# Batch norm's squares about a provisional mean, two output buffers and an early square root, in the last stage of a graph network on one core

## The chip, the cores and the metric

One Trainium2 chip, of which the kernel uses one core. The metric is the device time of the whole kernel in microseconds (us), the median of several executions. One execution was also taken by the hardware profiler; all rows of the trace below come from that one. Engines are called PE (TensorE), DVE (VectorE), ACT (ScalarE), POOL (GpSimd) and SP (SyncE, which here only issues transfers).

## What is computed

Three attention layers (GATv2) and then one edge-conditioned convolution (GINE), over a graph of 6,250 nodes with 64 channels and 200,000 edges sorted by destination. The change touches only the end of the last part, which is this:

```
agg = segment_sum(relu(x[src] + edge_attr @ W_edge.T + b_edge), dst)
h = x + agg
h = h @ W1.T + b1                    # 6250 x 64
mean = jnp.mean(h, axis=0)
var = jnp.var(h, axis=0)
h = gamma * (h - mean) * jax.lax.rsqrt(var + BN_EPS) + beta
h = jax.nn.relu(h)
out = x_before + (h @ W2.T + b2)
```

## The kernel before

Nodes lie on 128 partitions by 49 columns. They are worked on in seven groups (GROUPS = 7) of seven blocks (GB = 7) of 128 nodes. Edges are handled in 98 turns per layer; the three attention layers and the convolution each run through all of them. There is no scheduler: each engine has its own program, written out by hand, and the engines meet at semaphores. An engine runs its program in the order in which it is written, so a wait holds back all that stands behind it on that engine.

What follows the last turn is called the end stage here. It has two parts.

**First part, by groups, as gathers come in.** POOL issues 49 indirect transfers (L465), one per block, that fetch each node's summed messages. When the seven of a group have landed, DVE adds them to `h` (L1295, semaphore `s_z`). PE turns the group's seven blocks (L620, "T" below, semaphore `s_zT`, into `pT`, which is the first half of the PSUM tensor `pG`). ACT copies them to `zT` (L644 with output `sb_wide`, two instructions of 512 and 384 columns, "C", semaphore `s_zTc`). PE multiplies by W1 (L626, "M", semaphore `s_u`, into `pP`, the second half of `pG`). ACT adds the bias and writes `uT` (L870, two instructions, "I", semaphore `s_uc`). `zT` and `uT` both lie in the tensor `sb_wide`.

**Second part, over all nodes.** DVE sums `uT` by groups (L1304, seven instructions, and L1305 for the last column of the first 27 blocks), sums the sums (L1306) and scales them to minus the mean (L1310, semaphore `s_mean`). ACT squares `uT` about that mean into `zT`, a group at a time (L876, "S", semaphore `s_sq`); DVE sums the squares in the same way and scales them (L1313). ACT takes the root (L878), DVE makes the scale and bias (L1315 to L1319), ACT applies them with ReLU, seven instructions (L882). PE multiplies each group by W2 (L636, into `pT`); DVE adds the input and the second bias (L1324, two instructions a group, semaphore `s_final`), and SP sends the group's rows out (L456). PE's product of group g waits until DVE is done with group g - 1, since both use `pT`.

On DVE's program the seven additions L1295 stand in one loop, and the loop of L1304 behind it:

```
for g in range(GROUPS):
    sl = slice(g * GB, (g + 1) * GB)
    dve.wait_ge(s_nrow[g], (LAYERS + 1) * (16 * GB))
    tt(h[:, sl, :], h[:, sl, :], node_rows[:, sl, 0:C], ALU.add).then_inc(s_z, 1)
```

Of the kernel before, what the change touches and what calls it, by code (L numbers as in the profile page):

```python
# [36 lines left out]
P = 128  # L37
N, C, H, O = 6250, 64, 4, 16
# [12 lines left out]
GB = 7  # L51
GROUPS = B // GB
# [15 lines left out]
EPS = 1e-5  # L68
SLOPE = 0.2
LAST_PAD = N - (P - 1) * B  # L70


def build(nc, t):
    with ExitStack() as ctx:
        def sb(name, shape, dt=F32):
            return ctx.enter_context(nc.sbuf_tensor("sb_" + name, shape, dt))

        def sem(name):
            return ctx.enter_context(nc.semaphore(name))
# [29 lines left out]
        with ExitStack() as early:  # L109
# [16 lines left out]
        at = PARTS * B * TW  # L126
# [23 lines left out]
        w2t = sb("w2t", [C, C])  # L150
# [59 lines left out]
        zT = wide[0:C, 0:NB]  # L210
        uT = wide[0:C, NB:2 * NB]

        pG = ctx.enter_context(nc.psum_tensor("pG", [P, 4, 512], F32))
        pT, pP = pG[:, 0:2, :], pG[:, 2:4, :]
        pB = ctx.enter_context(nc.psum_tensor("pB", [P, 2048], F32))
        xr = pB[:, 0:C * G].rearrange("p (c g) -> p c g", g=G)
        at = C * G
# [8 lines left out]

        hT = xl[0:C, 0].rearrange("p g c -> p (g c)")[:, 0:GB * P].rearrange("p (i q) -> p i q", i=GB)
        bn = sb("bn", [C, 10])
        group_sum = sb("group_sum", [C, GROUPS + 1])


        s_x, s_const, s_dst, s_weights = sem("x_in"), sem("constants_in"), sem("dst_in"), sem("weights_in")
# [41 lines left out]
        s_u, s_uc, s_sq, s_bnstd, s_bnp, s_y = (sem(n) for n in (  # L274
            "u_product", "u_copied", "u_squared", "bn_std_ready", "bn_params", "y_ready"))
        s_mean = sem("mean_ready")
        s_o, s_final, s_result = sem("o_product"), sem("final_ready"), sem("result_out")
# [257 lines left out]
        def _(pe):  # L535
# [61 lines left out]
            with pe.Fori(0, PAIRS) as i:  # L597
                for k in range(2):
# [7 lines left out]
                    for q in range(2):  # L606
                        product = pe.matmul(pE[:, q * 512:(q + 1) * 512], attr[:, k, q * P:(q + 1) * P], w_blk[:, :],
                                        start=True, stop=True)
# [6 lines left out]
            for g in range(GROUPS):  # L615
# [3 lines left out]
                for i in range(GB):  # L619
                    product = pe.transpose(place(pT, i)[0:C, :], h[:, g * GB + i, :], ident[:, :])  # L620
# [4 lines left out]
                for half, (lo, n) in enumerate(((0, 4), (4, 3))):  # L625
                    product = pe.matmul(pP[0:C, half, 0:n * P], w1t[:, :], zT[:, (g * GB + lo) * P:(g * GB + lo + n) * P],  # L626
                                        start=True, stop=True)
                product.then_inc(s_u, 1)

            for g in range(GROUPS):  # L630
                pe.wait_ge(s_y, g + 1)
                if g:
                    pe.wait_ge(s_final, g)
                for i in range(GB):
                    b = g * GB + i
                    product = pe.matmul(pT[:, i // 4, (i % 4) * P:(i % 4) * P + C], zT[:, b * P:(b + 1) * P], w2t[:, :],  # L636
                                        start=True, stop=True)
                product.then_inc(s_o, 1)

# [2 lines left out]
        def _(act):  # L642
            def copy(out, in_):
                return act.activation(out, in_, ACT.Copy)  # L644
# [76 lines left out]
            def hand_out_linear(all_done, stored, turn, k):  # L721

                act.wait_ge(s_sums, all_done)
                act.wait_ge(s_stored[k], stored)
                rows = turn_out[:, k].rearrange("p g r -> p (g r)")[:, 0:G * C]
                copy(rows.rearrange("p (g c) -> p g c", g=G), lin_run[:, :, 1:G1].rearrange("p c g -> p g c")).then_inc(s_out, 1)
                act.wait_ge(s_out, all_done)
                act.dma_start(agg_runs[:, bass.ds(turn * (G * C), G * C)], rows).then_inc(s_stored[k], 16)
# [132 lines left out]
                linear_turn(PAIRS - 1, k, last=True)  # L861
            hand_out_linear((LAYERS + 1) * TURNS, (LAYERS + 1) * (16 * PAIRS) - 16, TURNS - 1, 1)

            for g in range(GROUPS):
                act.wait_ge(s_zT, g + 1)
                copy(zT[:, g * GB * P:(g * GB + 4) * P], pT[0:C, 0, :])
                copy(zT[:, (g * GB + 4) * P:(g + 1) * GB * P], pT[0:C, 1, 0:3 * P]).then_inc(s_zTc, 1)
                act.wait_ge(s_u, g + 1)
                for half, (lo, n) in enumerate(((0, 4), (4, 3))):
                    ins = act.activation(uT[:, (g * GB + lo) * P:(g * GB + lo + n) * P], pP[0:C, half, 0:n * P],  # L870
                                           ACT.Identity, bias=cols[:, 0:1])
                ins.then_inc(s_uc, 1)
            act.wait_ge(s_mean, 1)
            for g in range(GROUPS):
                sl = slice(g * GB * P, (g + 1) * GB * P)
                act.activation(zT[:, sl], uT[:, sl], ACT.Square, bias=bn[:, 2:3]).then_inc(s_sq, 1)  # L876
            act.wait_ge(s_bnstd, 1)
# [2 lines left out]
            for g in range(GROUPS):  # L880
                sl = slice(g * GB * P, (g + 1) * GB * P)
# [4 lines left out]
        def _(dve):  # L886
            tt, ts, cp, red = dve.tensor_tensor, dve.tensor_scalar, dve.tensor_copy, dve.tensor_reduce
# [7 lines left out]
            done, last, steps = chain(dve, s_pro)  # L895
# [348 lines left out]
            done, last, steps = chain(dve, s_pro, prologue_steps)  # L1244
# [47 lines left out]
            for g in range(GROUPS):  # L1292
                sl = slice(g * GB, (g + 1) * GB)
# [3 lines left out]
            u3 = uT.rearrange("c (b q) -> c b q", b=B)  # L1297
            z3 = zT.rearrange("c (b q) -> c b q", b=B)

            def node_sum(v3, ready):  # L1300

                for g in range(GROUPS):
                    dve.wait_ge(ready, g + 1)
                    done(red(group_sum[:, g:g + 1], v3[:, g * GB:(g + 1) * GB, 0:P - 1], AX.XY, ALU.add))  # L1304
                done(red(group_sum[:, GROUPS:], v3[:, 0:LAST_PAD, P - 1], AX.X, ALU.add)); last()  # L1305
                done(red(bn[:, 0:1], group_sum[:, :], AX.X, ALU.add)); last()  # L1306

            dve.wait_ge(s_weights, 16 * 9)
            node_sum(u3, s_uc)
            ts(bn[:, 2:3], bn[:, 0:1], -1.0 / N, None, ALU.mult).then_inc(s_mean, 1)  # L1310
            dve.wait_ge(s_mean, 1)
            node_sum(z3, s_sq)
            ts(bn[:, 4:5], bn[:, 0:1], 1.0 / N, EPS, ALU.mult, ALU.add).then_inc(s_bnstd, 1)  # L1313
            dve.wait_ge(s_bnstd, 2)
            done(dve.reciprocal(bn[:, 6:7], bn[:, 5:6])); last()  # L1315

# [3 lines left out]
            for g in range(GROUPS):  # L1320
                dve.wait_ge(s_o, g + 1)
                for half, (lo, n) in enumerate(((0, 4), (4, 3))):
                    sl = slice(g * GB + lo, g * GB + lo + n)
                    ins = tt(XR[:, sl, :], pT[:, half, 0:n * P].rearrange("p (i q) -> p i q", i=n)[:, :, 0:C], x[:, sl, :], ALU.add)  # L1324
                ins.then_inc(s_final, 1)


# [49 lines left out]
```

## Time and profile before

| | us |
|---|---|
| median of 3 executions | 6918.15 |
| lowest, highest | 6915.6, 6918.17 |
| the profiled execution, its own time | 6920.11 |
| the profiled execution, span from first to last instruction | 6918.3 |

The profiled execution's own time is 1.8 us above its span (what lies around the first and last instruction) and 2.0 us above the median. PE is busy for 80% of the span, DVE 73%, POOL 70%, ACT 68%, nearly all of it in the turns. The store of the last turn's sums is issued at 6793.6 us, so the end stage has the last 124 us or so, 1.8% of the span.

### The profile page before, as it was taken

Reading aid. Unit: us, or ns where it says so; the run is one execution under the profiler, and the core shown is the slowest. Engines: PE = TensorE matmul, PEld = TensorE weight load, DVE = VectorE, ACT = ScalarE, POOL = GpSimd, SP = SyncE. Lnnn points to the kernel's source line nnn. Section 1 sums busy time; section 2 is a strip of 40 time slices with the busy share of each in tenths; the row PEclk is TensorE's granted clock in tenths of the full one; section 3 lists DMA queues with packets and bytes.
Section 4 is the critical chain, followed back from the end, with each engine's and each line's share of the span. In section 5 each row is a group of like instructions: output and inputs, shape, how many; then the busy total and the mean of one; then the engine's idle time right before and its main releaser. Section 6 shows DMA issues by size and latency. Waiting matters only on the chain.

```text
span 6918.3 us, 90892 instructions
## 1 busy us (share of the span) xinstructions
PE 5522.5 (80%) x22976; PEld 4471.7 (65%) x22976; DVE 5033.6 (73%) x7664; ACT 4701.4 (68%) x6139; POOL 4844.1 (70%) x5111
## 2 busy tenths in 40 slices
PE   2588888888838888888855888888873999999995
PEld 1466666666627777777744777777762777777773
DVE  7588888888838988888865988888884434343442
ACT  0477777777727888888854888888871555555553
POOL 3666666666667777777767777777765777777774
PEclk9998999989959999999977999999996999999996
DMA  8444545445425555555533555555552444444441
GB/s 362 130 150 150 150 150 149 148 148 149 150 65 158 165 163 164 164 164 164 164 108 113 161 166 162 166 163 164 164 149 60 135 131 135 131 135 130 136 129 44
DMA packets 419825, 1018.62 MB, mean 147 GB/s; under 512 B 162514, under 2 KB 195268, under 8 KB 415446
## 3 DMA queue, kind: packets, MB, share of 16 engines
q1 hardware_dynamic: 198850, 612.23, 26.1%
q0 software_dynamic: 164208, 181.25, 14.2%
q10 hardware_dynamic: 56740, 224.88, 8.1%
q14 instruction: 23, 0.19, 0.0%
q8 instruction: 4, 0.07, 0.0%
HBM read 633.43 MB, written 384.49 MB: 147 GB/s over the span
## 4 chain that ended last, share of the span: by engine, by line
POOL 31%; issue 28%; DVE 18%; ACT 16%; ACTq 2%; PE 2%; DMA 1%; DVEq 1%; POOLq 0%; SPq 0%
POOL sb_xl L465 26%; ACT sb_turn_out L644 7%; DVE pG L1047 7%; DVE sb_s_run L1089 4%; POOL sb_hot_f L465 3%; ACT pB L644 3%; ACT sb_hot L644 3%; ACT sb_v_in L644 2%; POOL marks L469 2%; DVE sb_wide L1039 2%; DVE sb_s L1272 2%; PE pG L553 1%; DVE sb_mark L997 1%; ACT L644 1%; ACTq L718 1%
## 5 line engine op out<-in xcount | busy, mean ns | idle before, releaser
L553 PE MATMUL pG<-sb_xl_parts,sb_hot 128*128 128x476 f32 x21952 | 5187.1, 395 | 1110.5 <-ACT sb_xl L644 675.2
L465 POOL DMA_INDIRECT sb_xl<-xl_table,sb_idx x4704 | 4448.0, 946 | 1702.7 <-issue 1433.9
L553 PEld LDWEIGHTS pG<-sb_xl_parts,sb_hot 128*128 128x128 f32 x21952 | 4273.3, 197 | 2064.5 <-issue 1434.1
L1047 DVE COPY_PREDICATED pG<-sb_pick_turn,pG 128x408 f32<-128x408 int32 (+2 forms) x2352 | 1017.9, 435 | 1082.2 <-ACT sb_pick_turn L644 960.9
L644 ACT ACTIVATE sb_hot<-sb_wide 128x1792 fp32r<-128x1792 bf16 x784 | 1320.2, 1697 | 308.2 <-ACT sb_turn_out L644 287.3
L1089 DVE TENSOR_TENSOR_SCAN sb_s_run<-pB,sb_v_in 128x272 f32<-128x272 f32 (+2 forms) x1075 | 1083.9, 1016 | 24.4 <-ACT sb_turn_out L644 4.0
L644 ACT ACTIVATE sb_turn_out<-sb_s_run 128x1088 f32<-128x1088 f32 (+1 forms) x392 | 835.2, 2131 | 2.6 <-DVE sb_s_run L1089 2.6
L644 ACT ACTIVATE sb_xl<-pG 128x136 f32<-128x136 f32 (+2 forms) x826 | 243.1, 297 | 811.1 <-DVE pG L1047 724.9
L1086 DVE TENSOR_TENSOR_SCAN pB<-sb_same_c,pB 128x1024 f32<-128x1024 f32 x294 | 671.2, 2283 | 0.1
L644 ACT ACTIVATE sb_v_in<-sb_v_g 128x1024 f32<-128x1024 f32 x291 | 595.3, 2046 | 0.0
L644 ACT ACTIVATE pB<-sb_mark 128x960 f32<-128x960 f32 x294 | 551.5, 1876 | 12.4 <-DMA sb_mark<-marks 1.6
L644 ACT ACTIVATE sb_same_c<-sb_same 128x960 f32 (+1 forms) x294 | 306.3, 1042 | 285.9 <-issue 139.1
L1107 DVE TENSOR_TENSOR sb_s<-sb_xl,pB 128x1024 f32<-128x1024 f32 x294 | 357.8, 1217 | 145.7 <-DMA sb_xl<-xl_table,sb_idx 144.1
L1111 DVE TENSOR_REDUCE sb_e_in<-sb_lr 128x64 f32<-128x1024 f32 x294 | 359.1, 1222 | 10.1
L1109 DVE SCALAR_TENSOR_TENSOR sb_lr<-sb_s,pB 128x1024 f32<-128x1024 f32 x294 | 358.9, 1221 | 10.1
L1138 DVE TENSOR_TENSOR sb_v_g<-sb_xl,pB 128x1024 f32<-128x1024 f32 x291 | 355.2, 1220 | 10.0
L1039 DVE TENSOR_SCALAR sb_wide<-sb_wide,sb_code_no 128x512 bf16<-128x512 int16 x686 | 211.8, 378 | 3.7 <-DMA sb_wide<-codes 3.2
L844 ACT ACTIVATE sb_v_in<-sb_s 128x1024 f32<-128x1024 f32 x98 | 199.4, 2034 | 14.5 <-DVE sb_s L1272 1.3
L644 ACT ACTIVATE pB<-sb_same 128x544 f32 (+1 forms) x98 | 62.5, 638 | 211.3 <-DVE sb_s_run L1089 211.3
L469 POOL DMA_INDIRECT marks<-sb_XR,sb_first_edge x147 | 145.1, 987 | 72.5 <-issue 72.5
L644 ACT ACTIVATE sb_v_in<-sb_s_run 128x68 f32<-128x68 f32 (+1 forms) x389 | 125.4, 322 | 98.1 <-DVE sb_s_run L1089 97.8
L732 ACT ACTIVATE pB<-sb_wf_arg 128x576 f32<-128x576 f32 x294 | 187.1, 636 | 0.0
(199 smaller groups left out, 2278.9 us busy)
## 6 DMA issues: line engine op xcount, KB each, us to landing
sb_wide<-hots SPq DMA_DIRECT2D x294, 896.0 KB
state_rows<-sb_turn_out ACTq DMA_DIRECT2D x294, 576.0 KB
sb_mark<-marks SPq DMA_DIRECT2D x294, 512.0 KB
hots<-sb_wide SPq DMA_DIRECT2D x98, 896.0 KB, 4.0
sb_xl<-xl_table,sb_idx POOLq DMA_INDIRECT x4704
marks<-sb_hot_f SPq DMA_DIRECT2D x32, 1568.0 KB
agg_rows<-sb_turn_out ACTq DMA_DIRECT2D x98, 512.0 KB
sb_wide<-codes SPq DMA_DIRECT2D x98, 128.0 KB, 5.8
```

The source lines that it names most:

```text
L465: return pool.indirect_dma_start(out=dst, out_offset=None, in_=table, in_offset=bass.IndirectOffsetOnAxis(ap=index, axis=0))
L469: return pool.indirect_dma_start(out=table, out_offset=bass.IndirectOffsetOnAxis(ap=index, axis=0), in_=src, in_offset=None)
L553: product = pe.matmul(pG[:, a, 0:GB * TW], hot[k][:, m, a * P:(a + 1) * P], xl_part[part][:, m * GB * TW:(m + 1) * GB * TW], start=(m == 0 ...
L644: return act.activation(out, in_, ACT.Copy)
L1039: ins = ts(staged[k][:, m, :], code[k], code_no[:, m:m + 1], None, ALU.is_equal)
L1047: return dve.copy_predicated(rows[:, :, 0:n], over(pick_turn[:, k, stage, lo:hi], n), rows[:, :, at:at + n])
L1086: dve.tensor_tensor_scan(xr_flat, same_c[:].rearrange(flat3), xr_flat, 0.0, ALU.mult, ALU.add).then_inc(s_xr, 1)
L1089: return dve.tensor_tensor_scan(s_run[:, lo:hi, :].rearrange(flat3), factors[:, 0:(hi - lo) * G1], v_in[:, lo:hi, :].rearrange(flat3), 0.0 ...
L1107: tt(s[:], xl[:, k, :, 0:C], xr.rearrange("p c g -> p g c"), ALU.add).then_inc(s_added, 1)
L1109: done(dve.scalar_tensor_tensor(out=lr[:], in0=s[:], scalar=0.0, in1=blocks(a_turn, G), op0=ALU.max, op1=ALU.mult)); steps_done()
L1111: done(red(e_turn.rearrange("p h g -> p g h"), lr[:].rearrange("p g (h o) -> p g h o", h=H), AX.X, ALU.add)); steps_done()
L1138: tt(v_g[:].rearrange("p g (h o) -> p g h o", h=H), xl_heads, weights, ALU.mult).then_inc(s_used[k], 1)
```

## The change

There are three edits, all in the end stage.

1. **Squares.** ACT squares a group in the first part's loop, right after it has written the group's `uT`, about a provisional mean: that of the first group's columns alone (`bn[:, 2:3]`, made by DVE at L1311 from the first group's sum). DVE sums `uT` and the squares of a group in turn, and at the end corrects mean and variance for the provisional mean (L1313 to L1318).
2. **Output buffers.** The product by W2 uses the two halves of `pG` in turn for even and odd groups, and waits for the additions of group g - 2 in place of g - 1.
3. **Early root.** One `Sqrt` on a column of old data (`stat`) is put ahead of ACT's first part, with its result in a place that is overwritten later.

```diff
@@ tensor
             for g in range(GROUPS):
                 pe.wait_ge(s_y, g + 1)
-                if g:
-                    pe.wait_ge(s_final, g)
+                if g >= 2:
+                    pe.wait_ge(s_final, g - 1)
...
+                    at = 2 * (g % 2) + i // 4
-                    product = pe.matmul(pT[:, i // 4, (i % 4) * P:(i % 4) * P + C], zT[:, b * P:(b + 1) * P], w2t[:, :],
+                    product = pe.matmul(pG[:, at, (i % 4) * P:(i % 4) * P + C], zT[:, b * P:(b + 1) * P], w2t[:, :],
@@ scalar
+            act.activation(bn[:, 9:10], stat[0:C, 2, 0:1], ACT.Sqrt)
             for g in range(GROUPS):
                 act.wait_ge(s_zT, g + 1)
                 copy(zT[:, g * GB * P:(g * GB + 4) * P], pT[0:C, 0, :])
...
                 ins.then_inc(s_uc, 1)
-            act.wait_ge(s_mean, 1)
-            for g in range(GROUPS):
+                act.wait_ge(s_mean, 1)
+                act.wait_ge(s_uc, g + 1)
                 sl = slice(g * GB * P, (g + 1) * GB * P)
                 act.activation(zT[:, sl], uT[:, sl], ACT.Square, bias=bn[:, 2:3]).then_inc(s_sq, 1)
             act.wait_ge(s_bnstd, 1)
@@ vector
-            node_sum(u3, s_uc)
-            ts(bn[:, 2:3], bn[:, 0:1], -1.0 / N, None, ALU.mult).then_inc(s_mean, 1)
-            dve.wait_ge(s_mean, 1)
-            node_sum(z3, s_sq)
-            ts(bn[:, 4:5], bn[:, 0:1], 1.0 / N, EPS, ALU.mult, ALU.add).then_inc(s_bnstd, 1)
+            for g in range(GROUPS):
+                for a, (v3, ready) in enumerate(((u3, s_uc), (z3, s_sq))):
+                    dve.wait_ge(ready, g + 1)
+                    done(red(group_sum[:, a, g:g + 1], v3[:, g * GB:(g + 1) * GB, 0:P - 1], AX.XY, ALU.add))
+                    if g == LAST_PAD // GB:
+                        done(red(group_sum[:, a, GROUPS:], v3[:, 0:LAST_PAD, P - 1], AX.X, ALU.add))
+                    if g == 0 and a == 0:
+                        last()
+                        ts(bn[:, 2:3], group_sum[:, 0, 0:1], -1.0 / (GB * (P - 1)), None, ALU.mult).then_inc(s_mean, 1)
+            last()
+            done(red(bn[:, 0:2], group_sum[:, :, :], AX.X, ALU.add)); last()
+            done(dve.scalar_tensor_tensor(out=bn[:, 3:4], in0=bn[:, 0:1], scalar=1.0 / N, in1=bn[:, 2:3], op0=ALU.mult, op1=ALU.add)); last()
+            done(tt(bn[:, 8:9], bn[:, 3:4], bn[:, 3:4], ALU.mult))
+            done(tt(bn[:, 2:3], bn[:, 2:3], bn[:, 3:4], ALU.subtract)); last()
+            done(dve.scalar_tensor_tensor(out=bn[:, 1:2], in0=bn[:, 1:2], scalar=1.0 / N, in1=bn[:, 8:9], op0=ALU.mult, op1=ALU.subtract)); last()
+            ts(bn[:, 4:5], bn[:, 1:2], 1.0, EPS, ALU.mult, ALU.add).then_inc(s_bnstd, 1)
```

What each engine's program holds, before and after, is shown at three places. The first is ACT around the end of the turns. `sb_turn_out` is the last turn's result, `sb_wide` holds `zT` and `uT`, `z_turned` is `s_zT`, `u_product` is `s_u`, `u_copied` is `s_uc` and `mean_ready` is `s_mean`. Before:

```order
L728 DMA agg_rows<-sb_turn_out 128x1024 [waits turn_out_ready]
L644 ACTIVATE sb_wide<-pG 64x512 [waits z_turned]
L644 ACTIVATE sb_wide<-pG 64x384
L870 ACTIVATE sb_wide<-pG,sb_cols 64x512 [waits u_product]
L870 ACTIVATE sb_wide<-pG,sb_cols 64x384
L644 ACTIVATE sb_wide<-pG 64x512 [waits z_turned]
```

Of the change:

```order
L729 DMA agg_rows<-sb_turn_out 128x1024 [waits turn_out_ready]
L865 ACTIVATE sb_bn<-sb_stat 64x1
L645 ACTIVATE sb_wide<-pG 64x512 [waits z_turned]
L645 ACTIVATE sb_wide<-pG 64x384
L872 ACTIVATE sb_wide<-pG,sb_cols 64x512 [waits u_product]
L872 ACTIVATE sb_wide<-pG,sb_cols 64x384
L878 ACTIVATE sb_wide<-sb_wide,sb_bn 64x896 [waits u_copied,mean_ready]
L645 ACTIVATE sb_wide<-pG 64x512 [waits z_turned]
```

The square of the first group, with its wait for `mean_ready`, now stands between the first group's bias (L872) and the second group's copies (L645); the early root stands first. No load of an activation table stands here in either program; the last one is at L829 before and L830 after, ahead of the convolution's turns.

The second place is DVE from the first part's additions on (`sb_hot_f` holds the gathered rows, `sb_group_sum` the sums by group). Before:

```order
L1295 TENSOR_TENSOR sb_h<-sb_h,sb_hot_f 128x448 [waits node_rows_in5]
L1295 TENSOR_TENSOR sb_h<-sb_h,sb_hot_f 128x448 [waits node_rows_in6]
L1304 TENSOR_REDUCE sb_group_sum<-sb_wide 64x1 [waits u_copied,weights_in]
L1304 TENSOR_REDUCE sb_group_sum<-sb_wide 64x1 [waits u_copied] x6
L1305 TENSOR_REDUCE sb_group_sum<-sb_wide 64x1
```

Of the change:

```order
L1297 TENSOR_TENSOR sb_h<-sb_h,sb_hot_f 128x448 [waits node_rows_in5]
L1297 TENSOR_TENSOR sb_h<-sb_h,sb_hot_f 128x448 [waits node_rows_in6]
L1306 TENSOR_REDUCE sb_group_sum<-sb_wide 64x1 [waits u_copied,weights_in]
L1311 TENSOR_SCALAR sb_bn<-sb_group_sum 64x1 [waits dve_prologue_steps]
L1306 TENSOR_REDUCE sb_group_sum<-sb_wide 64x1 [waits u_squared]
L1306 TENSOR_REDUCE sb_group_sum<-sb_wide 64x1 [waits u_copied]
```

The scaling that releases `mean_ready` (L1311) now follows the first sum, where before six more sums stood ahead of it (L1310). The additions of all seven groups still stand ahead of the first sum.

The third place is PE's product by W2 (`y_ready` is counted up by ACT's ReLU, `final_ready` is `s_final`). Before:

```order
L636 MATMUL pG<-sb_w2t,sb_wide 128x64 [waits y_ready]
L636 MATMUL pG<-sb_w2t,sb_wide 128x64 x6
L636 MATMUL pG<-sb_w2t,sb_wide 128x64 [waits final_ready,y_ready]
L636 MATMUL pG<-sb_w2t,sb_wide 128x64 x6
L636 MATMUL pG<-sb_w2t,sb_wide 128x64 [waits final_ready,y_ready]
```

Of the change:

```order
L637 MATMUL pG<-sb_w2t,sb_wide 128x64 [waits y_ready]
L637 MATMUL pG<-sb_w2t,sb_wide 128x64 x6
L637 MATMUL pG<-sb_w2t,sb_wide 128x64 [waits y_ready]
L637 MATMUL pG<-sb_w2t,sb_wide 128x64 x6
L637 MATMUL pG<-sb_w2t,sb_wide 128x64 [waits final_ready,y_ready]
```

The second group's product no longer waits for DVE, and each later one waits for the addition before the last. What surrounds these places stands as it was.

## Rows read from the trace of the kernel before

**Rows 1.** The page: shares of the chain that ended last, by engine

```profile
POOL 31%; issue 28%; DVE 18%; ACT 16%; ACTq 2%; PE 2%; DMA 1%; DVEq 1%; POOLq 0%; SPq 0%
```

**Rows 2.** Timeline: start us, us, engine, instruction, count, idle before; first two groups

```profile
6814.73 0.96 ACT L644 ACTIVATE sb_wide<-pG 64x512 f32<-64x512 f32 x2 [21.22 <-PE pG L620]
...
6819.03 1.15 ACT L870 ACTIVATE sb_wide<-pG,sb_cols 64x512 f32<-64x512 f32 x2 [3.33 <-PE pG L626]
...
6821.43 0.62 DVE L1295 TENSOR_TENSOR sb_h<-sb_h,sb_hot_f 128x448 f32<-128x448 f32 x1 [8.49 <-DMA sb_hot_f<-agg_rows,sb_last_edge]
...
6822.11 1.70 PE L620 MATMUL pG<-sb_ident,sb_h 128*64 128x128 f32 x7 [3.12 <-DVE sb_h L1295]
```

**Rows 3.** Timeline of DVE, PE and ACT from the last group to the ReLU

```profile
6867.14 0.63 DVE L1295 TENSOR_TENSOR sb_h<-sb_h,sb_hot_f 128x448 f32<-128x448 f32 x1 [8.53 <-DMA sb_hot_f<-agg_rows,sb_last_edge]
6867.68 5.99 DVE L1304 TENSOR_REDUCE sb_group_sum<-sb_wide 64x1 f32<-64x889 f32 x6
...
6869.56 0.96 ACT L644 ACTIVATE sb_wide<-pG 64x512 f32<-64x512 f32 x2 [3.71 <-PE pG L620]
...
6870.58 3.24 PE L626 MATMUL pG<-sb_wide,sb_w1t 64*64 64x512 f32 x4 [1.05 <-ACT sb_wide L644]
...
6873.86 1.15 ACT L870 ACTIVATE sb_wide<-pG,sb_cols 64x512 f32<-64x512 f32 x2 [3.33 <-PE pG L626]
...
6876.25 0.15 DVE L1306 TENSOR_REDUCE sb_bn<-sb_group_sum 64x1 f32<-64x8 f32 x1
6876.44 0.14 DVE L1310 TENSOR_SCALAR sb_bn<-sb_bn 64x1 f32<-64x1 f32 x1
6876.62 6.64 ACT L876 ACTIVATE sb_wide<-sb_wide,sb_bn 64x896 f32<-64x896 f32 x7 [1.61 <-DVE sb_bn L1310]
6877.76 6.98 DVE L1304 TENSOR_REDUCE sb_group_sum<-sb_wide 64x1 f32<-64x889 f32 x7 [1.18 <-ACT sb_wide L876]
...
6885.07 0.14 DVE L1313 TENSOR_SCALAR sb_bn<-sb_bn 64x1 f32<-64x1 f32 x1
6885.25 0.20 ACT L878 ACTIVATE sb_bn<-sb_bn 64x1 f32<-64x1 f32 x1 [1.99 <-DVE sb_bn L1313]
...
6886.23 7.28 ACT L882 ACTIVATE sb_wide<-sb_wide,sb_bn 64x896 f32<-64x896 f32 x7 [0.78 <-DVE sb_bn L1319]
```

**Rows 4.** Timeline of PE and DVE in the product by W2

```profile
6887.42 3.25 PE L636 MATMUL pG<-sb_w2t,sb_wide 64*128 64x64 f32 x14 [13.60 <-ACT sb_wide L882]
...
6891.53 3.21 PE L636 MATMUL pG<-sb_w2t,sb_wide 64*128 64x64 f32 x14 [0.87 <-ACT sb_wide L882]
...
6894.79 0.69 DVE L1324 TENSOR_TENSOR sb_XR<-pG,sb_x 128x256 f32<-128x256 f32 x2 [3.40 <-PE pG L636]
...
6911.97 3.21 PE L636 MATMUL pG<-sb_w2t,sb_wide 64*128 64x64 f32 x14 [0.87 <-DVE sb_XR L1324]
```

**Rows 5.** Line L636: duration of one, ns, min/median/max

```profile
L636 PE MATMUL pG<-sb_w2t,sb_wide x98: 417/417/471, 6887.4 to 6914.8; 64*128 64x64 f32 x98
```

**Rows 6.** PE's timeline in the first layer's tables

```profile
50.43 0.64 PE L570 MATMUL pB<-sb_w_gat,sb_xl 64*128 x2
51.01 1.70 PE L564 MATMUL pG<-sb_ident,sb_h 128*64 128x128 f32 x7
```

**Rows 7.** Line L829, the last table load: duration ns, start us

```profile
L829 ACT ACT_TABLE_LOAD  x1: 1283/1283/1283, 5196.7 to 5196.7; - x1
```

**Rows 8.** Windows: busy us of PE, PEld, DVE, ACT, POOL; PEclk; DMA share; GB/s

```profile
5302.00:5308.00 6.00, 5.07 (x13) 4.32 (x14) 4.56 (x3) 1.03 (x1) 5.09 (x4) 0.50 0.09 17
5308.00:5310.00 2.00, 2.00 (x11) 1.76 (x10) 0.00 (x0) 2.00 (x2) 1.70 (x2) 1.00 0.19 35
6749.00:6757.00 8.00, 7.39 (x31) 5.42 (x30) 6.11 (x9) 2.46 (x7) 6.15 (x7) 1.00 0.27 75
6815.00:6819.00 4.00, 3.24 (x4) 0.73 (x4) 0.00 (x0) 0.70 (x2) 2.84 (x4) 0.50 0.11 25
6887.00:6915.00 28.00, 22.35 (x98) 21.39 (x98) 4.13 (x12) 6.51 (x7) 0.00 (x0) 0.50 0.13 49
```

**Rows 9.** Timeline: an edge product in the turns

```profile
6749.43 1.88 PE L607 MATMUL pB<-sb_w_blk,sb_wide 128*128 128x512 f32 x4
```

More of the change, by code:

```diff
@@ L228, in build @@
         bn = sb("bn", [C, 10])
-        group_sum = sb("group_sum", [C, GROUPS + 1])
+        group_sum = sb("group_sum", [C, 2, GROUPS + 1])
         s_x, s_const, s_dst, s_weights = sem("x_in"), sem("constants_in"), sem("dst_in"), sem("weights_in")
@@ L1298, in _ @@
             z3 = zT.rearrange("c (b q) -> c b q", b=B)
-            def node_sum(v3, ready):
-                for g in range(GROUPS):
+            dve.wait_ge(s_weights, 16 * 9)
+            for g in range(GROUPS):
+                for a, (v3, ready) in enumerate(((u3, s_uc), (z3, s_sq))):
                     dve.wait_ge(ready, g + 1)
[L1304 to L1308, printed above, removed]
-            node_sum(u3, s_uc)
-            ts(bn[:, 2:3], bn[:, 0:1], -1.0 / N, None, ALU.mult).then_inc(s_mean, 1)
-            dve.wait_ge(s_mean, 1)
-            node_sum(z3, s_sq)
-            ts(bn[:, 4:5], bn[:, 0:1], 1.0 / N, EPS, ALU.mult, ALU.add).then_inc(s_bnstd, 1)
+                    done(red(group_sum[:, a, g:g + 1], v3[:, g * GB:(g + 1) * GB, 0:P - 1], AX.XY, ALU.add))
[11 more added lines that the diff above has]
+            ts(bn[:, 4:5], bn[:, 1:2], 1.0, EPS, ALU.mult, ALU.add).then_inc(s_bnstd, 1)
             dve.wait_ge(s_bnstd, 2)
@@ L1323, in _ @@
                     sl = slice(g * GB + lo, g * GB + lo + n)
-                    ins = tt(XR[:, sl, :], pT[:, half, 0:n * P].rearrange("p (i q) -> p i q", i=n)[:, :, 0:C], x[:, sl, :], ALU.add)
+                    ins = tt(XR[:, sl, :], pG[:, 2 * (g % 2) + half, 0:n * P].rearrange("p (i q) -> p i q", i=n)[:, :, 0:C], x[:, sl, :], ALU.add)
                 ins.then_inc(s_final, 1)
```

## The prediction, made before the changed kernel had run

> **What bounds the kernel now.** I read the page's chain first, only to see where not to look: of the chain that ended last, 31% is POOL and 28% issue, the gathers of the turns, and the change touches none of it [rows 1]. All three edits lie in the last 124 us, so I read those in order of time, and the question at each edit is who ends the wait there. A change of 0.2% of 6918 us, 13.8 us, is about what a measurement of this kernel can tell from none.
>
> In the first part the gathers set the pace. DVE's addition of the second group waits 8.49 us for a transfer, and PE, behind it, 3.12 us for DVE [rows 2]. ACT is done with the first group at 6819.03 + 1.15 = 6820.18, over a microsecond before the second group's addition starts at 6821.43 [rows 2]. So C, M and I of groups 0 to 5 are hidden under POOL's gathers, and only the last group's are on the path: addition at 6867.14, C at 6869.56, M at 6870.58, I from 6873.86 to 6875.01 [rows 3].
>
> From there the second part is a chain of DVE and ACT: the last sum and its scaling, squares and their sums from 6876.62 to 6884.74, the root, then the ReLU at 6886.23, which is 11.22 us after I [rows 3]. The product by W2 is a ring of PE and DVE: PE starts a group every (6911.97 - 6891.53) / 5 = 4.09 us, works 3.21 and is idle 0.87 while DVE adds for 0.69 [rows 4].
>
> **Edit 1, the squares: first what stands ahead of the new wait.** The first square waits for `s_mean`. L1311 makes it from DVE's first sum, which stands, by DVE's order, behind the additions of all seven groups. The last of those waits for the last gather and starts at 6867.14; the first sum follows at 6867.68 in the trace of before [rows 3], though its data has been there since 6820.18 [rows 2]. Nothing in the change moves it. So L1311 comes at about 6868.8, not early, and ACT stands at its wait from 6820.18 on. Behind that wait on ACT are C and I of groups 1 to 6; behind the second group's C are M of the second group and, on PE's program, T and M of all the later ones. Neither DVE's additions nor POOL wait for ACT here, so the gathers go on as before, and nothing is deadlocked; but the first part, which the gathers hid, now begins again at group 1 when they are over.
>
> The start of that: first sum at 6867.68, 1.06 long (the pass over the squares has seven in 6.98 with the same shape; spaced 0.99), 0.04 to the next instruction (L1306's 0.15 from 6876.25 and L1310 at 6876.44), 0.14 for the scaling, 0.04 to ACT (L876 at 6876.62): S of group 0 at 6868.96 [rows 3]. Seven squares take 6.64, and the isolated one before DVE's sum takes 1.14 to be read (6876.62 to 6877.76), so they are spaced 6.64 less 1.03, over six: 0.935 [rows 3]. C of group 1 starts at 6869.90 and lasts 0.96, M follows 0.06 later (6869.56 + 0.96 to 6870.58): M of group 1 at 6870.92 [rows 3].
>
> One group's step from then on, M to M: M 3.24, 0.04, I 1.15, 0.04 for the new wait on `s_uc`, S 0.935, C 0.96, 0.06, together **6.43 us** [rows 3]. T (1.70, [rows 2]) runs beside I and S, which take 2.17 with their gaps, so it is hidden. If PE needed some 0.15 more ahead of T, as between the last L570 at 50.43 + 0.43 and the next transposes at 51.01 [rows 6], it would still be (1.85 against 2.17). M of group 6 starts at 6870.92 + 5 x 6.43 = 6903.07 and its I ends 4.43 later, at 6907.50. Before it was 6875.01. **Cost: 32.5 us.** The new wait on `s_uc`, which no row shows as such, is the least sure part of a step: between 0, as back-to-back instructions, and 0.2 a time, so the cost lies between 32.3 and 33.5; I take 0.04, as same-engine waits on DVE show.
>
> **What edit 1 gives back.** After the last I, only the last group's square and sum remain: S at 6907.54 for 1.03, sum of squares to 6909.67 (1.06 each; the sum of `uT` runs beside S). Then L1313, of 64x2 where L1306 of 64x1 takes 0.15 [rows 3], and five small operations of which no row shows the three-operand form; as the L1306, L1310 and L1313 rows they take 0.15 and 0.04 between them, one pair without a wait, so that L1318 starts at 6910.55. From L1313 before to the ReLU was 6886.23 - 6885.07 = 1.16 [rows 3], which gives the ReLU at 6911.71: 4.21 us after I, where before it was 11.22. **Gain: 7.0 us**, with bounds 6.0 (each small operation half as dear again and more) and 7.5 (they overlap).
>
> **Edit 2, the output buffers.** DVE's 0.69 leaves the ring. A group has 14 records over 3.21 with the last 0.417 long [rows 4, 5], so they are spaced (3.21 - 0.417) / 13 = 0.215 and 14 of them take 3.01. To that I add the 0.15 at a boundary whose wait is already met [rows 6]: 3.16 a group in place of 4.09. ACT's ReLU (7.28 for seven) and DVE's 0.69 are both shorter than that per group. Six steps: **gain 5.5 us**, with bounds 0 (another wait takes DVE's place) and 6.4 (no gap at all).
>
> **Edit 3, the early root.** What could be gained is a table load, 1.28 us by its row [rows 7]. But the root at L878 takes 0.20 and DVE goes on at once after it, no load stands ahead of it in the trace [rows 3], and the last load is the one at L829 1,690 us earlier [rows 7]. So there is nothing left to load ahead: **0**. The added instruction itself lies in ACT's idle time of 21.22 us before the first C [rows 2]; without that cover it would cost 0.2. The Trainium skill (ScalarE: Activation LUTs, What ACT_TABLE_LOAD costs) gives about 1283 ns for a load, and this trace agrees, 1283; its section on table sets says that cheap functions such as copy and relu are in every set, which fits the root's table staying loaded through the turns. Had a load stood at L878, the sum by that page would be better by 1.3 to 2.7 us, with the drain that it adds.
>
> **The sum.** 32.5 - 7.0 - 5.5 = +20.0 us. On the profiled execution's own time, 6920.1, that is 6940.1; on the median, which lies 2.0 lower, 6918.15 + 20 = **6938 us**, 0.29% slower.
>
> **The rivals.**
>
> *The clock rises (not slower).* The granted clock is 0.50, the 1.2 GHz level, at M and through the whole product by W2, where PE is busy 22.35 of 28 us. It rose to 1.00 (2.4 GHz) at the start of the convolution's turns, after PE had worked without a pause for about 5 us [rows 8]. With two buffers PE works through, and M and T now stand together for 4.94 us in each step. At 1.00 four records of 512 columns take 1.88 [rows 8, 9], M's 1,792 columns so 1.65, 1.6 less than now. If every step of the first part had it, that is 9.6 us; in the product by W2, at half of 3.16 after two slow groups, four steps and the last group, 7.9. Together 20.0 - 17.5: +2.5, **6921**. It decides from 6.2 us on, four fast M's or four fast groups. Against it: in the first layer's tables PE's small products and transposes stand together for about 5 us at a time, and a transpose there takes as long as in the end stage at 0.50: 1.70 for seven both times [rows 2, 6]. I give 4% to both places and 8% to the product by W2 alone, which gives +12.1, **6930**. The Trainium skill (TensorE: Matmul & The Clock Gate, What's actually happening) has it that "the default state is throttled, and activity releases the throttle", which speaks for this rival more than my rows do; by it alone the sum would be that of 6930, or less. For the product by W2 before, at four fifths busy, the trace shows no release.
>
> *The squares do run with the gathers.* If the provisional mean came when the first group's data are there, the 32.5 would go and the rest stay: -12.5, **6906**, or 0.18% faster. It needs DVE's first sum ahead of its later additions, and the order of its program says otherwise. 3%.
>
> *The second buffer gives nothing* (PE's next group is held by something other than DVE): +25.5, **6944**. The 0.87 of idle ends with DVE's addition in every step but the first [rows 4], so 5%.
>
> **How the numbers follow.** My forecast, 6938 with its own range of 6935 to 6941, has 80%. The range from 6930 to 6944 takes in the clock's rise in the product alone and the case without a second buffer's gain, and leaves out the two rivals that hold 7%. Slower by over 0.2%: 80 + 5 and half of the 6930 case, less a little for sizes, 84%. Within 0.2%: the rest of the clock's cases and nearly all of the third rival, 14%. Faster: 2%.
>
> **What the changed kernel's trace would show.** ACT idle for about 48.8 us ahead of its first square, released by DVE's L1311 at about 6868.9; transposes of group 1 done early and its product M 48 us late; M then every 6.4 us; the first sum on DVE right behind the last addition, as now; 4.2 us from the last I to the ReLU; products by W2 every 3.2 us with no idle time on DVE's account; the early root at 0.2 us, no table load. It would be wrong if the square of the first group started before the last gather, or if the clock in the end stage stood at 1.00.

## The result and the profile after

The changed kernel's median is 6935.54 us (6934.06 to 6940.02, 9 runs), that of the kernel before 6915.94 (6913.11 to 6918.41, 9 runs): 19.6 us slower, a ratio of 1.0029 with a 95% interval of 1.0019 to 1.0039. The profiled execution took 6940.02 us, 19.9 more than that of before. The forecast was +20.0 us and, as a time, 6938 us with a range of 6935 to 6941. The measured 6935.54 lies at the lower edge of that range, because the median of the kernel before was 2.2 us lower over nine runs than over the three that the forecast started from.

The timeline of the changed kernel, from the first group to the second square; columns as in [rows 2]:

```profile
6815.86 0.97 ACT L645 ACTIVATE sb_wide<-pG 64x512 f32<-64x512 f32 x2 [20.71 <-PE pG L620]
...
6820.16 1.15 ACT L872 ACTIVATE sb_wide<-pG,sb_cols 64x512 f32<-64x512 f32 x2 [3.33 <-PE pG L626]
...
6867.89 0.63 DVE L1297 TENSOR_TENSOR sb_h<-sb_h,sb_hot_f 128x448 f32<-128x448 f32 x1 [8.50 <-DMA sb_hot_f<-agg_rows,sb_last_edge]
6868.43 1.06 DVE L1306 TENSOR_REDUCE sb_group_sum<-sb_wide 64x1 f32<-64x889 f32 x1
6869.53 0.15 DVE L1311 TENSOR_SCALAR sb_bn<-sb_group_sum 64x1 f32<-64x1 f32 x1
6869.71 1.04 ACT L878 ACTIVATE sb_wide<-sb_wide,sb_bn 64x896 f32<-64x896 f32 x1 [48.40 <-DVE sb_bn L1311]
6870.66 0.94 ACT L645 ACTIVATE sb_wide<-pG 64x512 f32<-64x512 f32 x2
...
6871.66 3.24 PE L626 MATMUL pG<-sb_wide,sb_w1t 64*64 64x512 f32 x4 [46.67 <-ACT sb_wide L645]
...
6874.83 1.70 PE L620 MATMUL pG<-sb_ident,sb_h 128*64 128x128 f32 x7
6874.94 1.15 ACT L872 ACTIVATE sb_wide<-pG,sb_cols 64x512 f32<-64x512 f32 x2 [3.33 <-PE pG L626]
...
6876.18 1.04 ACT L878 ACTIVATE sb_wide<-sb_wide,sb_bn 64x896 f32<-64x896 f32 x1
6877.13 0.95 ACT L645 ACTIVATE sb_wide<-pG 64x512 f32<-64x512 f32 x2
...
6878.13 3.25 PE L626 MATMUL pG<-sb_wide,sb_w1t 64*64 64x512 f32 x4 [1.60 <-ACT sb_wide L645]
```

The bracket of the first L878 is where the cost comes from: ACT stands still for 48.40 us, until DVE's L1311, which starts 1.64 us after the start of the last of the seven additions. Behind it PE stands idle for 46.67 us before its second product by W1, and the first part begins again. From then on the products of two groups start 6.47 us apart.

The end of the same timeline:

```profile
6907.30 1.15 ACT L872 ACTIVATE sb_wide<-pG,sb_cols 64x512 f32<-64x512 f32 x2 [3.34 <-PE pG L626]
6908.48 2.21 DVE L1306 TENSOR_REDUCE sb_group_sum<-sb_wide 64x1 f32<-64x889 f32 x2 [4.27 <-ACT sb_wide L872]
6908.55 1.04 ACT L878 ACTIVATE sb_wide<-sb_wide,sb_bn 64x896 f32<-64x896 f32 x1
6910.73 0.16 DVE L1313 TENSOR_REDUCE sb_bn<-sb_group_sum 64x2 f32<-64x16 f32 x1
...
6911.54 0.15 DVE L1318 TENSOR_SCALAR sb_bn<-sb_bn 64x1 f32<-64x1 f32 x1
6911.72 0.20 ACT L880 ACTIVATE sb_bn<-sb_bn 64x1 f32<-64x1 f32 x1 [2.14 <-DVE sb_bn L1318]
...
6912.71 7.28 ACT L884 ACTIVATE sb_wide<-sb_wide,sb_bn 64x896 f32<-64x896 f32 x7 [0.78 <-DVE sb_bn L1324]
...
6913.89 21.17 PE L637 MATMUL pG<-sb_w2t,sb_wide 64*128 64x64 f32 x98 [6.63 <-ACT sb_wide L884]
6917.18 0.69 DVE L1329 TENSOR_TENSOR sb_XR<-pG,sb_x 128x256 f32<-128x256 f32 x2 [4.51 <-PE pG L637]
...
6935.10 0.69 DVE L1329 TENSOR_TENSOR sb_XR<-pG,sb_x 128x256 f32<-128x256 f32 x2 [2.30 <-PE pG L637]
```

PE's 98 records of the product by W2 (each of the 49 products leaves two) were seven pieces with gaps before, some of them in [rows 4]. Now they are one piece of 21.17 us without a gap.

The two traces laid over each other, in us. The "last gather's addition" is the last L1295 or L1297, at 6867.14 before and 6867.89 after; the "last output addition" is DVE's last L1324 or L1329, at 6915.22 and 6935.10.

| stretch | before | after | difference |
|---|---|---|---|
| start of the last gather's addition to the end of the last I | 7.87 | 40.56 | +32.7 |
| end of the last I to the ReLU | 11.22 | 4.26 | -7.0 |
| ReLU to the start of the last output addition | 28.99 | 22.39 | -6.6 |

That is +19.1. The other 0.8 us of the two profiled executions lie ahead of the last gather's addition, where nothing but the early root was changed; it runs there in ACT's idle time.

### The profile page after: what moved, and what is told of

Same layout as the page of the kernel before. It is cut to its first block, busy times and chain, and to the rows that moved or that the text cites. A ratio compares the mean times of both kernels' runs of the same rounds, so it can differ in the third digit from the quotient of the medians.

```text
span 6938.2 us, 90901 instructions
## 1 busy us (share of the span) xinstructions
PE 5509.4 (79%) x22976; PEld 4465.1 (64%) x22976; DVE 5033.4 (73%) x7667; ACT 4702.2 (68%) x6140; POOL 4841.9 (70%) x5111
## 4 chain that ended last, share of the span: by engine, by line
POOL 31%; issue 28%; DVE 18%; ACT 17%; ACTq 2%; PE 2%; DMA 1%; DVEq 1%; POOLq 0%; SPq 0%
POOL sb_xl L465 26%; ACT sb_turn_out L645 7%; DVE pG L1049 7%; DVE sb_s_run L1091 4%; POOL sb_hot_f L465 3%; ACT pB L645 3%; ACT sb_hot L645 3%; ACT sb_v_in L645 2%; POOL marks L469 2%; DVE sb_wide L1041 2%; DVE sb_s L1274 2%; PE pG L553 1%; DVE sb_mark L999 1%; ACT L645 1%; ACTq L719 1%
## 5 line engine op out<-in xcount | busy, mean ns | idle before, releaser
L645 ACT ACTIVATE sb_hot<-sb_wide 128x1792 fp32r<-128x1792 bf16 x784 | 1320.2, 1697 | 309.0 <-ACT sb_turn_out L645 287.4
L645 ACT ACTIVATE sb_turn_out<-sb_s_run 128x1088 f32<-128x1088 f32 (+1 forms) x392 | 836.6, 2134 | 2.6 <-DVE sb_s_run L1091 2.6
L645 ACT ACTIVATE sb_xl<-pG 128x136 f32<-128x136 f32 (+2 forms) x826 | 242.4, 296 | 808.3 <-DVE pG L1049 723.7
L645 ACT ACTIVATE sb_v_in<-sb_v_g 128x1024 f32<-128x1024 f32 x291 | 595.2, 2045 | 0.0
L645 ACT ACTIVATE pB<-sb_mark 128x960 f32<-128x960 f32 x294 | 551.5, 1876 | 12.8 <-DMA sb_mark<-marks 1.6
L645 ACT ACTIVATE sb_same_c<-sb_same 128x960 f32 (+1 forms) x294 | 306.0, 1041 | 286.6 <-issue 139.4
L645 ACT ACTIVATE pB<-sb_same 128x544 f32 (+1 forms) x98 | 62.5, 638 | 211.3 <-DVE sb_s_run L1091 211.3
L645 ACT ACTIVATE sb_v_in<-sb_s_run 128x68 f32<-128x68 f32 (+1 forms) x389 | 125.6, 323 | 98.4 <-DVE sb_s_run L1091 91.6
```

## The experiments

Times are medians against runs of the kernel before on the same chip; the intervals are those of the ratio. The kernel before took 6915.02, 6915.17 and 6922.15 us on the three chips of these runs, so a time is compared within its chip only. The section ends with a table of all runs by the rows of the end stage.

### Each edit alone

**Squares alone**: edit 1, without the other two. The edit is the squares' part of the diff above.

> Only edit 1 (the squares about the provisional mean), with one output buffer and no early root. My theory: the first square waits on ACT for a DVE sum that stands behind all additions, so groups 1 to 6 start again after the last gather. By the rows of the changed kernel (step 6.47 us from product to product, 21.17 us for the product by W2 in place of about 27.8), this costs about 19.6 + 6.6 = +26 us against the kernel before. The rival that the 19.6 us come from something else in the changed kernel (the buffers or the early root) expects about -7 here.

Measured: 6941.82 against 6915.17 us, **+26.7** (1.0038, 1.0024 to 1.0052; five runs). All of the loss is in this edit, and more than all. ACT's wait before the first square is there without the other two edits:

```profile
6865.27 1.04 ACT L876 ACTIVATE sb_wide<-sb_wide,sb_bn 64x896 f32<-64x896 f32 x1 [47.12 <-DVE sb_bn L1309]
```

**Buffers alone**, edit 2 on the kernel before:

```diff
-                if g:
-                    pe.wait_ge(s_final, g)
+                if g >= 2:
+                    pe.wait_ge(s_final, g - 1)
```

> Only edit 2 (two output buffers). My theory: PE's six steps of 4.09 us become about 2.99, -6.6 us. The rival in which the second buffer helps only behind the slower first part expects 0. The rival in which PE's clock rises, once PE works without a pause, expects -13 or less; the changed kernel's trace speaks against it (0.50 throughout).

Measured: 6908.08 us, **-7.1** (0.9990, 0.9981 to 1.0000). The interval of the time only just ends at 1, so the rows decide:

```profile
6884.42 21.16 PE L637 MATMUL pG<-sb_w2t,sb_wide 64*128 64x64 f32 x98 [13.60 <-ACT sb_wide L883]
```

One piece of 21.16 us, with DVE's additions 2.99 us apart in place of 4.09 and the clock at 0.50 all through. PE's ring loses DVE's part whatever stands ahead of it, and the clock's rival is out. By medians the two edits add up, 26.7 - 7.1 = 19.6, the whole change.

**Root alone**, edit 3 on the kernel before:

```diff
+            act.activation(bn[:, 9:10], stat[0:C, 2, 0:1], ACT.Sqrt)
```

> Only edit 3 (the early root). My theory: 0, within 1.5 us, since no table load stands at the root in the trace. The rival in which a load or its drain is hidden in the root's time expects -1.3 to -2.7; it is near what three rounds can tell, so the root's row and the rows around it decide: I expect 0.20 us for it with and without the early one.

Measured: 6915.70 us, **+0.5** (1.0001, 0.9991 to 1.0010). Times can't tell 0.5 from nothing; the rows can. ACT's timeline with the early root, its last column naming who ended the wait:

```profile
6791.29 0.20 ACT L864 ACTIVATE sb_bn<-sb_stat 64x1 f32<-64x1 f32 x1 [0.41 <-ACT sb_turn_out L644]
...
6880.78 0.20 ACT L879 ACTIVATE sb_bn<-sb_bn 64x1 f32<-64x1 f32 x1 [1.99 <-DVE sb_bn L1314]
6881.76 7.28 ACT L883 ACTIVATE sb_wide<-sb_wide,sb_bn 64x896 f32<-64x896 f32 x7 [0.78 <-DVE sb_bn L1320]
```

The root that matters takes 0.20 us and is followed by the ReLU 0.98 us after its start, both exactly as in [rows 3]. There was no load to take out of the way.

### Is it the order of DVE's program?

**Sums between the additions**: all three edits, but DVE sums group g - 1 right behind the addition of group g.

```diff
+            def group_sums(g):
+                for a, (v3, ready) in enumerate(((u3, s_uc), (z3, s_sq))):
...
             for g in range(GROUPS):
                 sl = slice(g * GB, (g + 1) * GB)
                 dve.wait_ge(s_nrow[g], (LAYERS + 1) * (16 * GB))
                 tt(h[:, sl, :], h[:, sl, :], node_rows[:, sl, 0:C], ALU.add).then_inc(s_z, 1)
+                if g:
+                    group_sums(g - 1)
+            group_sums(GROUPS - 1)
```

> All three edits of the change, with one difference: on DVE the sums of group g - 1 (of u and of its squares, and the first group's scaling) stand right behind the addition of group g, in place of behind all seven additions. My theory: ACT's first square then starts at about 3 us after the first group's bias instead of 48, the first part hides under the gathers again, and the whole change is worth -7.0 - 6.6 = -13.6 us against the kernel before, some 33 us less than the changed kernel. A rival: squares on ACT, 1 us for each group, and DVE's sums, 2 us for each, delay the last group's copies or addition; then it is -10 to -12. If the cost of the change lay not in the order of DVE's program, this kernel would stay at +20.

Measured: 6901.59 us, **-13.6** (0.9980, 0.9971 to 0.9990), and on another chip **-13.6** again, 6901.47 against 6915.02 (0.9980, 0.9971 to 0.9989). The change with its sums moved on one engine goes from 19.6 us slower to 13.6 faster. The first square, and the timeline around the last addition:

```profile
6822.44 1.04 ACT L878 ACTIVATE sb_wide<-sb_wide,sb_bn 64x896 f32<-64x896 f32 x1 [2.51 <-DVE sb_bn L1307]
...
6863.11 1.15 ACT L872 ACTIVATE sb_wide<-pG,sb_cols 64x512 f32<-64x512 f32 x2 [3.33 <-PE pG L626]
6864.35 1.04 ACT L878 ACTIVATE sb_wide<-sb_wide,sb_bn 64x896 f32<-64x896 f32 x1
...
6865.60 0.63 DVE L1312 TENSOR_TENSOR sb_h<-sb_h,sb_hot_f 128x448 f32<-128x448 f32 x1 [6.62 <-DMA sb_hot_f<-agg_rows,sb_last_edge]
6866.15 2.05 DVE L1302 TENSOR_REDUCE sb_group_sum<-sb_wide 64x1 f32<-64x889 f32 x2
```

ACT waits 2.51 us for the provisional mean in place of 48.40. The square of the last group but one is done before the last addition starts, and DVE still waits 6.62 us for a gather there: squares and sums of all groups but the last lie in the gathers' shadow.

**Only the first sum moved**: the first group's sum and L1311 stand behind the second addition, all other sums behind the seventh, as in the changed kernel.

```diff
+                if g == 1:
+                    dve.wait_ge(s_uc, 1)
+                    done(red(group_sum[:, 0, 0:1], u3[:, 0:GB, 0:P - 1], AX.XY, ALU.add)); last()
+                    ts(bn[:, 2:3], group_sum[:, 0, 0:1], -1.0 / (GB * (P - 1)), None, ALU.mult).then_inc(s_mean, 1)
```

> The changed kernel with one DVE pair moved: the first group's sum and the scaling that releases the first square stand behind the second addition; all the other sums stay behind the seventh. My theory: the wait of 48 us goes, and with it the 32.5 us of the restarted first part; in its place 13 sums of about 1 us stand behind the last addition (6867.7), so the ReLU comes some 7.9 us after the last bias in place of 4.2. Against the kernel before: -3.3 - 6.6 = -10 us, about 30 less than the changed kernel. The rival that what counts is to have the sums spread between the additions, not the place of the one wait, expects it near the changed kernel, +20.

Measured: 6912.13 against 6922.15 us, **-10.0** (0.9985, 0.9976 to 0.9995). Against the changed kernel's +19.6, one sum and one scaling, 1.2 us of work, in another place are worth 29.6 us. The first square now waits 3.08 us, and behind the last addition stand the other sums:

```profile
6828.49 1.04 ACT L878 ACTIVATE sb_wide<-sb_wide,sb_bn 64x896 f32<-64x896 f32 x1 [3.08 <-DVE sb_bn L1305]
...
6872.14 0.63 DVE L1301 TENSOR_TENSOR sb_h<-sb_h,sb_hot_f 128x448 f32<-128x448 f32 x1 [8.52 <-DMA sb_hot_f<-agg_rows,sb_last_edge]
6872.68 5.99 DVE L1311 TENSOR_REDUCE sb_group_sum<-sb_wide 64x1 f32<-64x889 f32 x6
...
6879.80 5.99 DVE L1311 TENSOR_REDUCE sb_group_sum<-sb_wide 64x1 f32<-64x889 f32 x6
...
6887.81 7.28 ACT L884 ACTIVATE sb_wide<-sb_wide,sb_bn 64x896 f32<-64x896 f32 x7 [0.78 <-DVE sb_bn L1326]
```

From the last I (6878.86 + 1.15 = 6880.01) to the ReLU it takes 7.80 us, as expected, 3.5 more than the 4.26 with the sums between the additions. That is what the place of the other sums costs.

### The clock in the end stage

The changed kernel's clock stayed at 0.50 through 21 us in which PE never paused. These runs ask why, with products that nobody reads (128x128 weights, 512 columns, into a free part of `pB`), all on the kernel with the sums between the additions.

**Warm in all of the first part**: two extra products behind each product by W1, six behind the last. **Warm at the end**: four behind the last alone.

```diff
                 product.then_inc(s_u, 1)
+                for _ in range(2 if g < GROUPS - 1 else 6):
+                    pe.matmul(pB[:, 0:512], w_blk[:, 0:P], w_blk[:, :], start=True, stop=True)
```

> The kernel with the sums between the additions, with extra products on PE that nobody reads (128x128 weights, 512 columns, into a free part of pB): two behind each group's product by W1, six behind the last. A question about the clock: if work without a pause of the large shape raises it to 1.00 in the end stage and the small products keep it there, the last group's transposes and product by W1 take 2.4 us less and the product by W2 about 10 less, -26 against the kernel before. If the clock falls again in the small products, -14 to -18. If it doesn't rise at all, the six extra products (10.2 us at 0.50) stand in the way of the product by W2 and the kernel is some 3 us slower than without them, -10.

> As the kernel with the sums between the additions, with four extra products (128x128 weights, 512 columns) behind the last group's product by W1 alone, in the time in which PE waits for the batch norm. At 0.50 they take 6.8 us, about the wait. If the clock rises after about 5 us of them and stays: about -8 to -10 against the kernel without them, -22 against the kernel before. If it doesn't rise or falls at once in the small products: 0 to +1 against the kernel without them, -13.

Measured: 6903.99 and 6904.89 against 6922.15 us, **-18.2** (0.9974, 0.9964 to 0.9984) and **-17.3** (0.9975, 0.9965 to 0.9984). Both miss the hopeful numbers, -26 and -22; the second also misses its other case, -13. Windows of the kernel that is warm at the end; columns as in [rows 8]:

```profile
6878.00:6880.00 2.00, 2.00 (x3) 0.75 (x3) 1.07 (x1) 1.88 (x3) 0.00 (x0) 0.50 0.00 0
6880.00:6882.00 2.00, 2.00 (x4) 0.70 (x3) 1.82 (x7) 0.00 (x0) 0.00 (x0) 0.52 0.00 0
6882.00:6884.00 2.00, 1.42 (x4) 0.35 (x2) 0.70 (x5) 1.10 (x2) 0.00 (x0) 1.00 0.00 0
6884.00:6886.00 2.00, 1.71 (x15) 1.71 (x16) 0.00 (x0) 2.00 (x3) 0.00 (x0) 1.00 0.00 0
6886.00:6888.00 2.00, 2.00 (x20) 2.00 (x20) 1.03 (x3) 2.00 (x3) 0.00 (x0) 1.00 0.16 61
6888.00:6890.00 2.00, 2.00 (x15) 2.00 (x14) 0.84 (x4) 2.00 (x3) 0.00 (x0) 0.69 0.46 169
6890.00:6894.00 4.00, 4.00 (x21) 4.00 (x20) 0.89 (x3) 0.39 (x1) 0.00 (x0) 0.50 0.15 57
```

The clock rises at about 6882, 4.3 us after the first extra product (6877.58). In the kernel without the extra products it stays at 0.50 all through the end stage, so they are what raised it. The small ones start at 6884.29, some 20 of them in 2 us where 0.50 allows about nine; and then, with PE busy in every microsecond, the clock falls at about 6889 and stays down to the end of the product by W2. It is not a pause of PE that brings it down here.

**One large product among the small**: one more extra product behind each of the first six groups of the product by W2, added to warm at the end ("keep, end") and to warm in all of the first part ("keep, all").

```diff
                 product.then_inc(s_o, 1)
+                if g < GROUPS - 1:
+                    pe.matmul(pB[:, 0:512], w_blk[:, 0:P], w_blk[:, :], start=True, stop=True)
```

> The kernel with four extra products behind the last product by W1, and one more extra product (128x128 weights, 512 columns) behind each of the first six groups of the product by W2. In the kernel without these six the clock fell from 1.00 to 0.50 about 5 us after the small products had begun, though PE was busy throughout. If what the clock wants is PE's work of the larger shape among the small, it stays at 1.00: seven groups of 1.5 and six extra products of 0.9 take about 16 us in place of 17.1, so about -1 against the kernel without the six, -22 against the sums between the additions is out of reach; about -18 against the kernel before. If it wants only a busy PE, the fall had another cause: the clock falls again, the extra products cost 1.7 each at 0.50, and the kernel is some 5 us slower than without them, -8 against the kernel before.

> All extra products together: two behind each group's product by W1, six behind the last, and one behind each of the first six groups of the product by W2. If the clock stays at 1.00 from the last transposes on: the last group's transposes and product by W1 up to 2.4 us shorter, the product by W2 about 16 us in place of 21.2: -18 to -20 against the kernel before. If it falls in the product by W2: about -12.

> The kernel with the sums between the additions once more, unchanged, on the same chip as the two kernels that add to it, so that the extra products can be weighed against it directly: -13.6 us against the kernel before, the product by W2 at 0.50 throughout in 21.17 us.

Measured against 6915.02 us: keep, all 6898.57, **-16.5** (0.9977, 0.9968 to 0.9986), 2.9 less than the sums between the additions on the same chip. Window of its product by W2, and the timeline of one group and its extra product:

```profile
6879.00:6897.00 18.00, 18.00 (x108) 12.83 (x108) 4.13 (x12) 5.43 (x6) 0.00 (x0) 1.00 0.21 77
```

```profile
6890.24 1.77 PE L639 MATMUL pG<-sb_w2t,sb_wide 64*128 64x64 f32 x14
6891.94 1.12 PE L643 MATMUL pB<-sb_w_blk 128*128 128x512 f32 x2
6893.00 1.77 PE L639 MATMUL pG<-sb_w2t,sb_wide 64*128 64x64 f32 x14
```

In this execution, with a large product among the small, the clock stays at 1.00 to the end. A group with its extra product takes 2.76 us (6890.24 to 6893.00), against 2.99 for the group alone at 0.50.

Keep, end: 6909.94, **-5.1** (0.9986, 0.9977 to 0.9995), but no single number describes it: of 11 executions five took 6896 to 6901 us and six 6910 to 6916. The profiled one is of the second kind. Its timeline of PE:

```profile
6879.34 1.77 PE L639 MATMUL pG<-sb_w2t,sb_wide 64*128 64x64 f32 x14 [1.81 <-ACT sb_wide L888]
6881.04 1.25 PE L643 MATMUL pB<-sb_w_blk 128*128 128x512 f32 x2
6882.23 3.25 PE L639 MATMUL pG<-sb_w2t,sb_wide 64*128 64x64 f32 x14
6885.40 2.07 PE L643 MATMUL pB<-sb_w_blk 128*128 128x512 f32 x2
```

Here PE had paused for 1.81 us between its extra products and the product by W2, and the clock fell during the first extra product of the product by W2, the one behind the first group (1.25 us in place of 1.12). From there a group with its extra product takes 5.18 us. The clock did not come back, though the same mix of products ran without a pause to the end; window of PE from the fall on:

```profile
6882.23:6911.30 29.07, 29.07 (x95) 20.84 (x94) 3.44 (x10) 3.21 (x4) 0.00 (x0) 0.50 0.13 48
```

So the larger shape among the small does not by itself give 1.00: the same mix ran at 1.00 in one execution and at 0.50 in another. The expectation's two cases both occurred, in different executions, the faster five at -15 to -19 us against the kernel before (expected -18), the slower six at -5 to +1 (expected -8). The clock goes with the time: averaged over the whole execution it was 0.919 to 0.920 in the five faster ones and 0.917 or 0.918 in the six slower. Of keep, all one execution in 11 took 6911 us, at 0.919 against 0.920 to 0.922 in the other ten. What decides between the two was not tried.

All runs by their rows: the time from the start of the last gather's addition to the start of DVE's last output addition in the one profiled execution of each, beside the medians.

| kernel | medians, against before | rows, us | against before |
|---|---|---|---|
| before | | 48.08 | |
| the change | +19.6 | 67.21 | +19.1 |
| squares alone | +26.7 | 73.81 | +25.7 |
| buffers alone | -7.1 | 41.47 | -6.6 |
| root alone | +0.5 | 48.08 | 0.0 |
| sums between the additions | -13.6, -13.6 | 34.52, 34.52 | -13.6 |
| only the first sum moved | -10.0 | 38.06 | -10.0 |
| warm in all of the first part | -18.2 | 30.75 | -17.3 |
| warm at the end | -17.3 | 30.48 | -17.6 |
| keep, end (a slower execution) | -5.1 | 45.38 | -2.7 |
| keep, all | -16.5 | 31.38 | -16.7 |

## Why the prediction was right

Point by point, the forecast's terms and what they measured:

| term | forecast | measured |
|---|---|---|
| ACT's wait before the first square | 48.8 us | 48.40 us |
| one step of the restarted first part | 6.43 us | 6.47 us |
| last I, later against the last addition | +32.5 us | +32.7 us |
| last I to ReLU | -7.0 us | -7.0 us |
| ReLU to last output addition (the buffers) | -5.5 us | -6.6 us |
| early root | 0 | 0.0 us by the rows of the root alone |
| sum | +20.0 us | +19.1 us by rows, +19.6 us by medians |

**The wait in front of the first square.** The step that carried the forecast was that L1311 stands behind all seven additions. The run with one sum moved shows it by itself: 29.6 us for one instruction pair in another place.

**What was luck.** The mechanism and the sizes of the first three terms are right, but the sum came nearer than its terms. The buffers gave 1.1 us more than forecast; the profiled executions' difference, 19.9, has 0.8 us back from a stretch ahead of the last gather's addition, and the medians' 19.6 some 0.5 us, which no term stood for.

**The step of 6.43.** It was put together from five durations and their gaps. The new wait on `s_uc`, for which no row stood, I took as 0.04; from the end of the bias to the square it is 0.09 us (6874.94 + 1.15 to 6876.18). That accounts for the 0.04 us by which a step was longer. Transposes were hidden, as said: 6874.83 + 1.70 is before the copies' 6877.13.

**What the edit gives back**: L1313 to L1318 take 0.14 to 0.16 us each with 0.03 to 0.04 between, the forms without a row included; one pair, L1315 and L1316, overlaps, as forecast.

**The buffers.** This term was mis-sized by 1.1 us. I had added 0.15 for the boundary between two groups, read off [rows 6], where the next group's instructions wait for other semaphores. Here 98 records go through at 0.214 us each from the first to the last, and a group takes 2.99 us (DVE's additions 6920.16, 6923.15 and on), not 3.16. The figure without a gap, 3.01, was the right one, and the measured 6.6 us lies just above the upper bound of 6.4 that the forecast gave this term.

**The rivals.** *The clock rises*: it did not, 0.50 over the 98 records and over the steps of 6.47. I had 12% on it, with [rows 2, 6] against it. [rows 6] counts by its durations alone: the profile's clock line reads 1.00 there (see the last section). The Trainium skill (TensorE: Matmul & The Clock Gate, What's actually happening) was in this rival's favour with "activity releases the throttle". The changed kernel does not agree: 21.17 us of PE without a gap stayed at 0.50. The measurement decides.

*The squares run with the gathers*: this is what the kernel with the sums between the additions does. Forecast -12.5, measured -13.6; the 1.1 us between them are the buffers' again. *The second buffer gives nothing*: 7.1 us by itself.

**The early root.** What the forecast's rows left open is why no load stood there. The last load, at L829, belongs to a line that is itself a `Sqrt` (`stat[:, 2, :]`, once ahead of the convolution's turns), and no load follows it in the trace.

## What to carry to other kernels

Before work is moved into a loop that waits for transfers, look in the program of the engine that releases it, not only in that of the engine that does it: an early result counts from when its producer's turn comes. A wait put into the middle of an in-order loop costs everything behind it that had been hidden, here 32.7 us for a wait in front of a square of 1.04 us. The whole change with that producer interleaved is worth 13.6 us, 7.0 of them the squares' by the rows (13.6 less the buffers' 6.6; they were not run without the buffers), so a slower result is no verdict on the idea.

An instruction that loads a table ahead is worth something only if a load stands in the trace at the place that is to be relieved.

## What was not expected of the hardware

**The clock fell under work.** PE's clock fell from 1.00 to 0.50 while PE was busy in every microsecond, in products with 64-row weights and 64 columns: 4.5 us after they began in warm at the end (6884.29 to about 6888.8) and 3.7 us after in warm in all of the first part (6879.57 to about 6883.2). With a product of 128x128 by 512 behind each group it stayed at 1.00 over 18 us in the profiled execution of keep, all. In the turns too, with products of 128x128 by 476, it stood at 1.00 in the window of [rows 8]. But in the profiled execution of keep, end the same mix, once the clock was down, ran for 29 us at 0.50. What the clock went by is not shown.

**What warmth bought.** Little is left of it: at 1.00 a group takes 1.56 us in place of 2.99 (between DVE's additions at 6886.10 and 6887.66 of warm at the end), but with the extra product that goes with it, it takes 2.76. All the extra products together gave 2.9 us on the same chip (6898.57 against 6901.47), with one execution in 11 at 6911 us. The best medians against their own chip's kernel before are -18.2 and -17.3, of the two kernels in which the clock fell; they ran on another chip than the kernel without extra products. By the rows of the table above, which leave out all that lies ahead of the end stage's last addition, warm at the end gives 4.0 us (30.48 against 34.52), warm in all of the first part 3.8, keep, all 3.1. Each is one execution.

**The clock line at the program's start.** In the first layer, where the profile gives a clock of 1.00, seven transposes take 1.70 us [rows 6], as long as in the end stage at 0.50. In keep, all, seven transposes at a recorded 1.00 take 0.95 us (6866.87). Window of the kernel before:

```profile
45.00:56.00 11.00, 8.56 (x38) 7.12 (x37) 10.68 (x19) 3.19 (x10) 1.34 (x2) 1.00 1.00 427
```

There the durations and the clock line don't agree, so near a program's start a clock is better read off the durations.
